# ScalarE's low-bit sum and the layernorm scaling of two chunks back exchange their places in the attention body

## The reference

```python
Q = _xpos(einsum('bld,hde->bhle', X, W_Q)); K = _xpos(einsum(..., W_K), downscale=True)
V = einsum('bld,hdv->bhlv', X, W_V)
scores = einsum('bhle,bhme->bhlm', Q, K) * D[None]        # D: causal decay mask
Y = einsum('bhlm,bhmv->bhlv', scores, V)
Yn = (Y - mean) * rsqrt(var + EPS) * gn_weight + gn_bias  # per head
out = G * sigmoid(G) * Yn @ W_O                           # G = X @ W_G
...
x = _layernorm(x + out)
```

## Time and profile before

| | |
|---|---|
| median of 3 runs | 1227.87 us (1227.55 to 1230.63) |
| the profiled execution | 1225.68 us, its span 1223.9 us |
| PE busy, share of the span | 1092.6 us, 89% |
| DVE busy | 966.1 us, 79% |
| ACT busy | 608.0 us, 50% |
| POOL busy | 485.0 us, 40% |

### The profile page before, as it was taken

How to read it: one execution, slowest core, us unless ns; L and a number is a source line. 1 busy time by engine, 2 the same in 40 slices (tenths; PEclk the granted TensorE clock), 3 DMA queues, 4 the chain that set the end, 5 groups by cost and what they waited for, 6 DMA issues and landing times.

```text
span 1223.9 us, 16462 instructions
## 1 busy us (share of the span) xinstructions
PE 1092.6 (89%) x5760; PEld 844.9 (69%) x5760; DVE 966.1 (79%) x1414; ACT 608.0 (50%) x1041; POOL 485.0 (40%) x381
## 2 busy tenths in 40 slices
PE   7999999557999999999999999999999999994334
PEld 3666666345878777778778877877878887772323
DVE  4688888446104699899899899989989998998883
ACT  2345555324434535755565573566456447434453
POOL 1466666436334324424343432443443344331220
PEclk9999999869999999999999999999999999998657
DMA  7245544532342242144042323313414232310000
GB/s 238 104 163 174 186 177 178 179 121 97 124 135 86 86 137 87 52 118 141 18 138 70 120 86 98 125 51 106 138 48 120 86 103 67 106 52 1 0 17 17
DMA packets 45339, 127.01 MB, mean 104 GB/s; under 512 B 4321, under 2 KB 21473, under 8 KB 43105
## 3 DMA queue, kind: packets, MB, share of 16 engines
q1 hardware_dynamic: 44416, 114.72, 29.4%
q10 hardware_dynamic: 864, 11.54, 2.5%
HBM read 117.86 MB, written 19.92 MB: 113 GB/s over the span
## 4 chain that ended last, share of the span: by engine, by line
DVE 54%; PE 27%; issue 10%; ACT 6%; POOL 2%; DMA 0%; ACTq 0%; DVEq 0%; SPq 0%; POOLq 0%
PE lower L1154 7%; DVE tmp L2008 7%; PE lower L438 7%; DVE tmp L1998 6%; DVE Sq L2000 5%; DVE tmp L2014 4%; DVE delta L2010 4%; PE bank L1154 4%; PE lower L531 2%; DVE stats L140 2%; DVE delta L2012 2%; DVE S L2016 2%; ACT look L634 1%; PE lower L492 1%; PE bank L468 1%
## 5 line engine op out<-in xcount | busy, mean ns | idle before, releaser
L1820 POOL TENSOR_TENSOR a_lo<-whole,a_hi 128x512 fp32r<-128x512 f32 x128 | 182.4, 1443 | 272.6 <-ACT a_hi L1457 196.7
L1154 PE MATMUL lower<-b_hi,ring 128*128 128x512 f32 x512 | 193.3, 395 | 1.4 <-ACT a_hi L1457 1.4
L1154 PE MATMUL lower<-a_hi,ring 128*128 128x512 f32 x512 | 193.9, 397 | 0.3 <-issue 0.3
L1154 PE MATMUL lower<-b_lo,ring 128*128 128x512 f32 x512 | 190.4, 390 | 1.7 <-POOL b_lo L1820 1.7
L1154 PE MATMUL lower<-a_lo,ring 128*128 128x512 f32 x512 | 190.3, 389 | 0.0
L1820 POOL TENSOR_TENSOR b_lo<-whole,b_hi 128x512 fp32r<-128x512 f32 x64 | 93.8, 1474 | 143.6 <-ACT b_hi L1457 143.6
L1440 ACT ACTIVATE S<-S 128x1024 f32<-128x1024 f32 x56 | 58.6, 1058 | 183.3 <-DVE S L2016 183.3
L1456 ACT ACTIVATE whole<-lower,hs 128x512 f32<-128x512 f32 x128 | 87.7, 685 | 82.7 <-PE lower L1154 79.2
L438 PE MATMUL lower<-wa,xT 128*128 128x512 f32 x240 | 111.6, 609 | 9.7 <-DMA wa<-wa_dram 6.8
L1154 PEld LDWEIGHTS lower<-b_hi,ring 128*128 128x128 f32 x512 | 96.2, 188 | 21.7 <-issue 1.8
L1154 PEld LDWEIGHTS lower<-b_lo,ring 128*128 128x128 f32 x512 | 96.0, 188 | 21.8 <-POOL b_lo L1820 2.3
(11 more groups left out here) (258 smaller groups left out, 2368.1 us busy)
## 6 DMA issues: line engine op xcount, KB each, us to landing
ring<-ffn_copy_dram SPq DMA_DIRECT2D x128, 512.0 KB, 3.7
look<-ffn_dram ACTq DMA_DIRECT2D x6, 1879.0 KB, 6.9
ffn_copy_dram<-ffn_dram SPq DMA_DIRECT2D x8, 1408.0 KB, 9.4
xT<-xT_dram SPq DMA_DIRECT2D x8, 512.0 KB, 8.2
rope<-rope_dram SPq DMA_DIRECT2D x8, 512.0 KB, 8.3
xtok<-x_dram SPq DMA_DIRECT2D x8, 512.0 KB, 4.0
x1in<-x_dram SPq DMA_DIRECT2D x8, 512.0 KB, 4.9
x1res<-x_dram SPq DMA_DIRECT2D x8, 512.0 KB, 3.3
```

The source lines that it names most:

```text
L1154: ins = nc.tensor.matmul(out, a, b, start=(first and n == 0), stop=(last and n == len(pairs) - 1))
L1820: nc.gpsimd.tensor_tensor(lo[:, m, :], t["whole"][:, m % 4, :], hi[:, m, :].bitcast(F32), ALU.subtract).then_inc(lo_done, 1)
```

## The change

In ScalarE's body the two pieces change places. `add_low_bits(c - 1)` with its `look_load(c)` now stands behind `value_gate(n, other, 1)` and ahead of `first_copies(c, 0)`; `normalise(c - 2, parity)` now stands behind `y_copy(c, 0)` and ahead of `value_gate(n, other, 3)`. Nothing is added or left out, and the order on the other engines is the same.

```diff
@@ -640,19 +640,19 @@
                 if more:
                     value_gate(n, other, 1)
-                if follow and not (isinstance(c, int) and c == 1):
-                    normalise(c - 2, parity)
+                if follow and not (isinstance(c, int) and c > LOOKS):
+                    add_low_bits(c - 1)
+                    if not (isinstance(c, int) and c == LOOKS):
+                        act.wait_ge(low_added, c)
+                        look_load(c)
                 if attend:
                     first_copies(c, 0)
                 if more:
                     value_gate(n, other, 2)
                 if attend:
                     y_copy(c, 0)
-                if follow and not (isinstance(c, int) and c > LOOKS):
-                    add_low_bits(c - 1)
-                    if not (isinstance(c, int) and c == LOOKS):
-                        act.wait_ge(low_added, c)
-                        look_load(c)
+                if follow and not (isinstance(c, int) and c == 1):
+                    normalise(c - 2, parity)
                 if more:
                     value_gate(n, other, 3)
                 if follow:
```

## The result

The changed kernel takes 1220.82 us (1220.21 to 1222.2, 6 runs) where the kernel before takes 1227.71 us (1225.74 to 1230.63, 6 runs): a ratio of 0.9945, 95% interval 0.9932 to 0.9958. That is 6.9 us less, twice the 3.5 us forecast, and under 1222.3, the low end of the stated range.

A forecast was written before the change was run, and what follows sets the result against it. TensorE was taken to set the pace in bodies 1 to 5, losing time waiting for `zT`. Gains of 3.1 + 0.4 = 3.5 us took the median from 1227.87 to 1224.4 us, range 1222.3 to 1227.0.

The forecast's parts named there:

- the product no longer waits: TensorE's output product in the loop: its wait for `zT`, 0.66 us in body 3, goes whole.
- the third `v` waits for its projection: ScalarE's late place: normalisation ends at 133.34, so `v` can start when its projection is done, 134.18.
- `yT` and `look` have room: Early place: the sum, 4.07 us to the next work, delays `yT`, whose transposes leave 1.76 us in hand.
- the dead heat at GpSimd: GpSimd's first state update, at 127.45, against ScalarE's copy ending at 127.39: 0 to 0.1 us a body, uncovered 0.4 us.
- VectorE didn't take the gain: Residual in the loop: VectorE and GpSimd would leave 1.0 of TensorE's 3.1 us, giving 1226.5 us; chance 10%.
- the slower cases: Above the forecast: transfers reach both holes, 1226.3 us, 10%; sum holds up `yT`, 1234.4, 4%; change does nothing, 1227.5, 3%.
- Gain: 0.38 + 2.7 = 3.1 us over five bodies.: TensorE's waits for `zT` ahead of the output product: 0.38 us in body 1 and 2.7 over four bodies, all recovered.
- Bounds: 1.9 us either way; I take 0.: Body 6: shifting SyncE's transfers some 4 us might move contention between GpSimd's two holes, 1.9 us either way; taken as 0.
- rival 1: Body 6: the transfers' new place also shortens GpSimd's holes, say 1.5 us more, up to 5.4 in all: 1222.9 us; chance 15%.
- The prediction's own sign of being wrong: GpSimd in body 6: the forecast is wrong if its two holes add up to something well off 16.8 us.
- Bounds 0 and 0.4; I take 0.4.: Body 6: the sum is done earlier, so VectorE's `low_all` starts 0.38 us sooner and GpSimd's hole ahead of the reduction follows.

The follow-up runs named there:

- the loop alone: Kernel before, with the two pieces exchanged in bodies 1 to 5 only and body 6 in the old order: 1222.57 us, ratio 0.996.
- body 6 alone: Kernel before, with the two pieces exchanged in body 6 only and the loop in the old order: 1224.57 us, ratio 0.9974.
- both pieces early: Against the changed kernel, the scalings return to their early place with the low-bit sum right behind them, late place empty: 1224.23 us, ratio 0.9981.
- the last kernel: Changed kernel with GpSimd's reduction moved behind group_root(6, 0) and five loads issued ahead of SyncE's store: 1204.48 us, ratio 0.9817.

## Why the prediction was wrong

The direction held, and so did the steps of the exchange inside a body: the product no longer waits, the third `v` waits for its projection, `yT` and `look` have room, the dead heat at GpSimd cost nothing, VectorE didn't take the gain, and none of the slower cases came. Three terms of the sum were off.

1. **"Gain: 0.38 + 2.7 = 3.1 us over five bodies."** Mis-sized: it measured 4.4 us (151.18 - 146.82), shown by the spacing of the products with the loop alone. The bracket ahead of a pipelined matmul is the idle time between a modelled end and a start. When the wait goes, the next group also starts before that end (0.15 us of overlap) and runs 0.10 us shorter. The trace of before had most of it: its last two products, with no wait ahead of the last, start 227.46 - 197.83 = 29.63 us apart and the others 30.4.
2. **"Bounds: 1.9 us either way; I take 0."** This is the step that failed in kind. The transfers' shift was worth 2.2 us of gain: 4.05 off the first hole, 1.83 onto the second. The shift itself was as the prediction had it, some 4 us against the hole (`x1in` from 2.2 us ahead of its start to 1.7 behind); its price was not. The cause was named as rival 1, with 15% and a gain of 1.5 us, 1.9 at most. The bound came from the difference of the two holes in one trace, as if both were the same work. Undisturbed they are not: with the loads held or issued early the first took 5.7 to 5.8 us and the second 7.2 to 7.4, so contention had cost the first 4.1 us and not 1.9. The prediction's own sign of being wrong came with it: the two holes add up to 5.79 + 9.22 = 15.01 us and not 16.8.
3. **"Bounds 0 and 0.4; I take 0.4."** Measured 0: the hole starts when GpSimd is free, as the held loads showed. The Trainium skill (GPSIMD Engine Reference, Instruction dispatch) gives about 6 us for the code loading of a fresh GpSimd function; the undisturbed 5.7 to 5.8 us agree. It counts them without the event wait, and I took that for a load that starts behind the wait; here what fills the hole ran beside the wait. That it is code loading no run here shows: in the kernel before with its loads held, the trace has no transfer packet from 226.7 to 242 us, in either hole.

So 3.1 + 0.4 + 0 = 3.5 should have read 4.4 + 0 + 2.2 = 6.6. The range failed since its low end, 1222.3 us, took in rival 1 at its full 5.4 us and little more.

Open is why a hole is slowed by such different amounts under much the same transfers. The stretches of the changed kernel (columns as in the earlier trace rows):

```profile
222.00:225.00 3.00, 3.00 (x24) 2.87 (x23) 1.94 (x4) 2.88 (x7) 0.00 (x0) 1.00 0.48 183
225.00:228.00 3.00, 2.83 (x16) 2.25 (x14) 0.00 (x0) 0.14 (x1) 0.32 (x1) 1.00 0.91 328
```

The first hole, 221.89 to 227.68, had 91% DMA share in its second half and stayed at 5.79 us. What differs is when the `x1in` load goes out, with the loads behind it. It was 1.7 us behind the hole's start in the changed kernel, with body 6 alone and with the loads moved forward (5.79, 5.61 and 5.72 us). It was 0.8, 1.3, 1.8 and 2.2 us ahead of it with the loop alone, with the reduction moved, with both pieces early, and before the change (11.25, 10.64, 9.87 and 9.84 us). In the last kernel it was 0.7 us ahead, but with one load behind it and not six (6.99 us). That the hole's first few us are the sensitive ones fits this, but no run varied that distance alone, and among the four long holes the length doesn't grow with it.

## What to carry to other kernels

Price a removed wait by the spacing of the work around it, from start to start, and look in the same trace for a turn of the loop where the wait is absent; here the idle time in the bracket, 0.66 us, was less than the 0.91 that came back. When an edit on one engine moves a semaphore that a transfer queue waits for, follow the whole queue: here seven loads behind one store were worth a third of the gain. And where an engine stands still on both sides of an instruction, look first at whether the critical chain has to run through that place at all; moving the reduction behind one instruction was worth 11 us, more than the exchange.

## What the runs showed of the hardware

- GpSimd's idle stretch ahead of `partition_all_reduce` lasted 5.6 to 5.8 us when SyncE's loads were held or went out behind its start (or five of them well ahead of it), 7.0 us when two loads went out about its start, and 9.8 to 11.3 us when all seven were going out as it began.
- The one behind it, ahead of an ordinary GpSimd operation, lasted 6.7 to 7.4 us with next to no transfers in it, and 9.1 to 10.2 us with transfers in its first 5 to 7 us (9.22 in the changed kernel, 9.12 with body 6 alone, 9.24 and 10.22 with the reduction moved).
- Behind the branch TensorE sat idle for 5.6 to 7.8 us and again for 1.6 to 2.1 us; with 2.7 MB of loads beside it the second stretch grew to 3.6 and 4.3 us. With the reduction moved, TensorE had no work left when the flag came, and its first work followed the flag's end by 7.8 and 7.7 us.
- The granted TensorE clock fell to 0.5 in the 14 to 19 us of standstill in body 6. In the kernel before it was back at 1.0 from 272 us on, in the changed kernel from 264 us on.
